# First scatters of a routed expert layer in threes, and a second routing choice made earlier

## The reference, cut to what matters

```
u     = xn2 @ (Ws + Wi).T + bs + bi        # xn2: a second layernorm with weight and bias
h_t   = tanh(h_(t-1) @ A.T + u_t)          # a recurrence of width 16 over 2048 steps
s     = (H @ Wo.T + bo) * sigmoid(xn2 @ Wg.T + bg) + xn
score = sigmoid(xn @ gate_w.T)             # 16 experts
idx   = top4(score + gate_b); w = 2.5 * score[idx] / sum(score[idx])
y     = sum_k w_k * (silu(gate) * up) @ w2[idx_k].T + shared expert(xn)
out   = x + s * silu(y)
```

## Time and profile before

| | us |
|---|---|
| median of three runs | 548.22 |
| lowest, highest run | 541.35, 548.29 |
| the profiled execution, its own time | 537.79 |
| its span, first to last instruction | 535.6 |

### The profile page before, as it was taken

The page is one execution under the profiler, slowest core; times in us unless marked ns, Lnnn a source line. Parts: engine busy times, 40 slices in busy tenths (PEclk is TensorE's granted clock), DMA queues, the critical chain, the costliest instruction groups (busy, mean ns, idle before and its releaser), DMA issues.

```text
span 535.6 us, 11523 instructions
## 1 busy us (share of the span) xinstructions
PE 375.5 (70%) x3635; PEld 294.3 (55%) x3635; DVE 307.3 (57%) x913; ACT 280.8 (52%) x532; POOL 265.5 (50%) x280
## 2 busy tenths in 40 slices
PE   0458357697998988769888898997867778673110
PEld 0344225265887877647666786776756556551000
DVE  4889637277752456523554567776643445456544
ACT  1842548567765454546666677766745444451000
POOL 2007746660005666565665554545456555425774
PEclk9977779699999899888999999999989788787555
DMA  7988967964868897588878898988867777345454
GB/s 243 386 279 306 303 229 227 357 189 132 249 216 258 261 298 224 168 267 253 264 238 280 263 301 279 273 272 262 262 197 249 219 208 217 121 144 165 145 153 129
DMA packets 106569, 127.06 MB, mean 237 GB/s; under 512 B 10257, under 2 KB 95890, under 8 KB 106514
## 3 DMA queue, kind: packets, MB, share of 16 engines
q1 hardware_dynamic: 92544, 92.17, 53.7%
q0 software_dynamic: 12288, 33.57, 20.7%
q10 hardware_dynamic: 1682, 0.59, 0.4%
HBM read 59.71 MB, written 66.58 MB: 236 GB/s over the span
## 4 chain that ended last, share of the span: by engine, by line
PE 40%; issue 13%; DVE 9%; POOL 5%; ACT 5%; another core or an unknown queue 3%; DMA 1%; POOLq 0%; ACTq 0%; DVEq 0%
PE bank L739 16%; PE bank L762 10%; PE bank L563 6%; POOL xn_parts L544 5%; PE bank L752 4%; ACT xn_f L1588 2%; DVE xn_parts L1322 2%; DVE xn_f L1271 1%; DVE sh_h L1277 1%; DVE sh_silu L1285 1%; PE bank L786 1%; ACT xn_f L1596 1%; PE bank L791 1%; PE bank L840 1%
## 5 line engine op out<-in xcount | busy, mean ns | idle before, releaser
L523 POOL DMA_INDIRECT x_slots<-xn_parts,slot_u x128 | 129.2, 1009 | 154.6 <-PE bank L563 67.3
L544 POOL DMA_INDIRECT xn_parts<-y_slots,slot_u x128 | 129.3, 1010 | 108.6 <-PE bank L563 29.5
L739 PE MATMUL bank<-w_all,xn_f 128*128 x1038 | 139.4, 284 | 17.2 <-issue 13.5
L1271 DVE SCALAR_TENSOR_TENSOR xn_f<-bank,xn_f 128x256 f32<-128x256 f32 x88 | 36.9, 419 | 152.0 <-ACT xn_f L1596 90.3
L739 PEld LDWEIGHTS bank<-w_all,xn_f 128*128 128x128 f16 x1038 | 100.7, 102 | 40.5 <-issue 26.7
L1588 ACT ACTIVATE xn_f<-bank 128x1024 f16<-128x1024 f16 x88 | 88.5, 1007 | 26.3 <-remote 15.9
L1612 ACT ACTIVATE y_ring<-bank 128x512 f32<-128x512 f32 x88 | 51.9, 590 | 68.7 <-PE bank L762 40.1
L762 PE MATMUL bank<-w_all,sh_silu 128*128 x519 | 76.5, 285 | 9.2 <-issue 7.3
L563 PE MATMUL bank<-ident_h,w_stage 128*128 128x128 f16 x692 | 56.4, 225 | 2.9 <-issue 1.9
L762 PEld LDWEIGHTS bank<-w_all,sh_silu 128*128 128x128 f16 x519 | 47.8, 103 | 18.7 <-issue 11.8
L1596 ACT ACTIVATE xn_f<-bank 128x256 f32<-128x256 f32 x88 | 33.5, 381 | 44.5 <-remote 21.4
(11 more groups left out here) (173 smaller groups left out, 479.4 us busy)
## 6 DMA issues: line engine op xcount, KB each, us to landing
w_stage<-x_slots SPq DMA_DIRECT2D x85, 256.0 KB
y_slots<-y_ring SPq DMA_DIRECT2D x85, 256.0 KB
x_ring<-in_x SPq DMA_DIRECT2D x32, 256.0 KB
x_slots<-zero_h SPq DMA_DIRECT2D x1, 8064.0 KB, 30.6
x_slots<-zero_h SPq DMA_DIRECT2D x7, 1024.0 KB
x_slots<-zero_h SPq DMA_DIRECT2D x7, 768.0 KB
w_stage<-in_w13t SPq DMA_DIRECT2D x17, 256.0 KB
x_ring<-in_x SPq DMA_DIRECT2D x8, 512.0 KB
```

The source lines that it names most:

```text
L523: eng.indirect_dma_start(out=x_slots[s], out_offset=bass.IndirectOffsetOnAxis(ap=slot_u[:, n * TOPK + k:n * TOPK + k + 1], axis=0), in_=xn ...
L544: eng.indirect_dma_start(out=fin_y[:, r, j, k, :], out_offset=None, in_=y_slots[s], in_offset=bass.IndirectOffsetOnAxis(ap=slot_u[:, n * T ...
L739: mm = eng.matmul(gu[:, j * 2 * F:(j + 1) * 2 * F], xg_T[:, n % 2, ((j * 2 + px) * KD + k) * P:((j * 2 + px) * KD + k + 1) * P], w_all[:, ...
L1271: eng.scalar_tensor_tensor(out=h_sb[:, n % 2, 0:nb, :], in0=gv[:, 0:nb, F:2 * F], scalar=DESCALE, in1=silu_sb[:, n % 2, 0:nb, :], op0=ALU. ...
```

## The change

It does six things. (1) POOL no longer scatters segment 0 tile by tile: the 48 scatters go in sixteen groups of three, and each group but the first waits for a step of a list (`steps`), the last of them `gate_pre` 14. (2) Of the preparation in the head, batch 7 moves one loop later on each engine: x_norm from loop 3 to 4, x_low from 4 to 5, transposes and scoring from 5 to 6. (3) VectorE chooses the experts of group 3 in loops 3 and 4 of the head and of group 4 in loop 5, no longer in slots 3 to 14 of the pairs; only group 5 stays there. (4) Ranks, counts and slots of segment 1 come in slots 7 to 19 and no longer 10 to 25. (5) Scatters of segment 1 start at pair count 9 and spread over 20 counts (before 11 and 17), those of segment 2 at 29 and over 16 (before 28 and 14). (6) Gathers and units move by up to three pairs to later ones, and gathers of segment 1 spread slightly wider.

```diff
--- before.py
+++ after.py
@@ -80,10 +80,13 @@
     FIN_RING = 3
     XF_RING = 2
     XM_RING = 2
-    SCATTER_PAIR = (0, 11, 28)
-    SCATTER_PAIRS = (0, 17, 14)
+    SCATTER_PAIR = (0, 9, 29)
+    SCATTER_PAIRS = (0, 20, 16)
     PIECES = 8
-    GATE_LEAD = 2
+    NORM_AT = {0: 4, 1: 5, 2: 6, 4: 7}
+    LOW_AT = {0: 3, 1: 4, 2: 5, 3: 6, 5: 7}
+    TURN_AT = {1: 3, 2: 4, 3: 5, 4: 6, 6: 7}
+    ROW = 3
 
     ctx = ExitStack()
     with ctx:
@@ -311,9 +314,9 @@
         SCAN0 = [U_SLOT + 4, U_SLOT + 4 + 25]
         OUT_SLOT = 43
         CHECK, FALLBACK, PARTS = U_SLOT + 55, U_SLOT + 59, U_SLOT + 60
-        UNIT_PAIR = (46, 50, 55, 59, 64, 68, 74, 77, 80, 83)
-        GATHER_PAIR = (43, 47, 52, 56, 61, 65, 70, 73, 76, 79, 82, 85)
-        GATHER_PAIRS = (4, 3)
+        UNIT_PAIR = (48, 52, 56, 60, 64, 68, 74, 78, 81, 85)
+        GATHER_PAIR = (45, 49, 53, 57, 61, 65, 70, 74, 77, 81, 84, 88)
+        GATHER_PAIRS = (8, 7)
         UNIT_SLOT = {SLOTS * p: c for c, p in enumerate(UNIT_PAIR)}
         MIX_SLOT = {78 + 6 * c: c for c in range(NU)}
 
@@ -497,16 +500,15 @@
             eng.wait_ge(diagonal, 3)
             eng.memset(shift_f[:, P // SEQS:P // SEQS + N], 0.0).then_inc(shifted, 1)
 
-            def beside_gates(n):
-
-                if n == 1:
-                    eng.wait_ge(sh_silu_done, 1)
-                elif n == 2:
-                    eng.wait_ge(sh_hidden, 1)
-                elif n == 3:
-                    eng.wait_ge(sh_lo, 1)
-                elif n > 3:
-                    eng.wait_ge(gate_pre, n - GATE_LEAD)
+
+            steps = ((sh_silu_done, 1), (sh_hidden, 1), (gate_pre, 2), (x_hi, 5), (gate_pre, 3), (x_hi, 6), (gate_pre, 5),
+                     (x_hi, 7), (gate_pre, 7), (gate_pre, 8), (gate_pre, 9), (gate_pre, 10), (gate_pre, 11),
+                     (gate_pre, 13), (gate_pre, 14))
+
+            def beside_gates(i):
+                if i and i % ROW == 0:
+                    made, count = steps[i // ROW - 1]
+                    eng.wait_ge(made, count)
 
             def slot_x(s):
                 eng.wait_ge(filled[s], 16 * (1, PIECES, PIECES)[s])
@@ -514,9 +516,9 @@
                     if n in GRP0:
                         eng.wait_ge(slots_step, 4 * GRP0.index(n) + 4)
                     b = n // BT
-                    if s == 0:
-                        beside_gates(n)
                     for k in range(TOPK):
+                        if s == 0:
+                            beside_gates(n * TOPK + k)
                         if s:
                             i = (n - TILE0[s]) * TOPK + k
                             eng.wait_ge(pair_t, SCATTER_PAIR[s] + i * SCATTER_PAIRS[s] // (SEG_TILES[s] * TOPK))
@@ -540,7 +542,7 @@
                     n = c * FT + j
                     if c < len(GATHER_PAIR):
                         i = k * FT + j
-                        eng.wait_ge(pair_t, GATHER_PAIR[c] + i * GATHER_PAIRS[s] // (TOPK * FT))
+                        eng.wait_ge(pair_t, min(GATHER_PAIR[c] + i * GATHER_PAIRS[s] // (2 * TOPK * FT), NPAIR))
                     eng.indirect_dma_start(
                         out=fin_y[:, r, j, k, :], out_offset=None, in_=y_slots[s],
                         in_offset=bass.IndirectOffsetOnAxis(ap=slot_u[:, n * TOPK + k:n * TOPK + k + 1], axis=0))\
@@ -690,12 +692,12 @@
             bias_products()
             blocks_ended(0)
             for b in range(NB):
-                if 0 < b < NB - 2:
-                    x_transpose(b + 2)
+                if b in TURN_AT:
+                    x_transpose(TURN_AT[b])
                 shared_up(b)
                 gates(b, 0)
-                if 0 < b < NB - 2:
-                    route_batch(b + 2)
+                if b in TURN_AT:
+                    route_batch(TURN_AT[b])
                 if b < NB - 1:
                     gates(b, 1)
 
@@ -844,14 +846,14 @@
             def beside(slot):
                 if slot == 1:
                     u_transpose()
-                if slot == 10:
+                if slot == 7:
                     rank(3)
-                if slot == 14:
+                if slot == 8:
                     rank(4)
                     block_counts(1)
-                if slot == 16:
+                if slot == 10:
                     block_starts(1)
-                if slot == 23:
+                if slot == 17:
                     blocks_ended(1)
                 if slot == 38:
                     rank(5)
@@ -1195,8 +1197,8 @@
                 if b == 1:
                     norm_stats(6)
                 shared_hidden(b)
-                if b + 3 < NB:
-                    x_low(b + 3)
+                if b in LOW_AT:
+                    x_low(LOW_AT[b])
                 if b == NB - 1:
                     u_ratio(0)
                 gates(b, 0)
@@ -1211,6 +1213,14 @@
                     norm_stats(7)
                     norm_scale(3)
                     norm_ratio(3)
+                if b == 3:
+                    choose_scores(3)
+                    choose_largest(3)
+                    choose_index(3)
+                if b == 4:
+                    choose_marks(3)
+                if b == 5:
+                    choose(4)
             u_ratio(1)
             def pick_weights(i):
                 r = slice(i * GT, (i + 1) * GT)
@@ -1368,26 +1378,25 @@
                     out_weights()
                 if slot == OUT_SLOT + 6:
                     out_bias()
-                for g, first in ((3, 3), (4, 7), (5, 27)):
-                    if slot == first:
-                        choose_scores(g)
-                    if slot == first + (1 if g < 5 else 3):
-                        choose_largest(g)
-                    if slot == first + (3 if g < 5 else 6):
-                        choose_index(g)
-                    if slot == first + (4 if g < 5 else 9):
-                        choose_marks(g)
-                for s, counts in ((1, 15), (2, 39)):
+                if slot == 27:
+                    choose_scores(5)
+                if slot == 30:
+                    choose_largest(5)
+                if slot == 33:
+                    choose_index(5)
+                if slot == 36:
+                    choose_marks(5)
+                for s, counts in ((1, 9), (2, 39)):
                     if slot == counts:
                         block_counts(s)
                     if slot == counts + 2:
                         block_starts(s)
-                for g, first in ((3, 18), (4, 20), (5, 42)):
+                for g, first in ((3, 12), (4, 14), (5, 42)):
                     if slot == first:
                         route_slots(g)
                     if slot == first + 1:
                         route_rows(g)
-                for s, first in ((1, 22), (2, 44)):
+                for s, first in ((1, 16), (2, 44)):
                     if slot == first:
                         blocks_ended(s)
                     if slot == first + 3:
@@ -1544,18 +1553,18 @@
             x_norm(3)
             weights_high(0)
             for b in range(NB):
-                if 0 < b < NB - 2:
-                    x_transposed(b + 2)
-                    x_low_transposed(b + 2)
+                if b in TURN_AT:
+                    x_transposed(TURN_AT[b])
+                    x_low_transposed(TURN_AT[b])
                 shared_up(b)
                 weights_high(2 * b + 1)
                 shared_hidden(b)
-                if 0 < b < NB - 2:
-                    route_batch(b + 2)
+                if b in TURN_AT:
+                    route_batch(TURN_AT[b])
                 weights_high(2 * b + 2)
                 gates(b, 0)
-                if b + 4 < NB:
-                    x_norm(b + 4)
+                if b in NORM_AT:
+                    x_norm(NORM_AT[b])
                 if b < NB - 1:
                     gates(b, 1)
 
```

## The result

| | before | after |
|---|---|---|
| median of four runs each, same chip | 544.79 (540.49 to 548.29) | 521.54 (520.55 to 522.21) |
| ratio, with its 95% interval | | 0.9575 (0.9482 to 0.9668) |
| the profiled execution, its own time | 537.79 | 521.4 |
| its span | 535.6 | 519.1 |

The account below looks back on a forecast made before the run. No single bound: a head, 88 pairs paced mostly by TensorE, then POOL's gathers and the last units. Terms 5 + 2 - 5 - 2 - 1 + 0 = -1 us gave 547.2 on the median, put at 546; range 535 to 557.

Parts of the forecast that it names:

- (a): Handover to the pairs: segment 0's last scatters become late and delay the first load of x slots; +5 us (+3 to +8).
- (c): Head, up to 72 us and 88 to 110: twelve fewer scatters where the standstills lie; -5 us (bounds 0 and -16).
- +2 for the choosing: Head, loops 3 to 6: choosing for groups 3 and 4 partly sticks out, batch 7 moves; +2 us (0 to 4).
- rival 2: Head: both standstills go, 16 us less in place of 5, giving 536; chance 0.13.
- (d): Pairs 3 to 8: the choosing leaves the pairs, so they run faster; -2 us (0 to -2.5).
- (e): Pairs: segment 1's scatters spread over 20 pair counts instead of 17; -1 us (bounds +2 and -14.5).
- Rival 3: Segment 1: density of scatters decides its pace, -14.5 us instead of -1, about 534; chance 0.07.
- (f): Late pairs: gathers and unit slots move later, last unit still fits POOL's idle time; 0 us, up to +2.

Follow-up runs that it names:

- bursts: The changed kernel with the same scatters and gathers over the same pairs, but released eight at a time: 647.56 us, ratio 1.1864.
- the thin ones: The bursts kernel with one eighth of each row moved by its indirect transfers: 641.90 us, ratio 1.1935.

## Why the prediction was wrong, step by step

**(a) to (c), the handover.** The sum came near and its parts did not; that was in part luck. I had +5 for the late scatters, +2 for the choosing, -5 for the stretches, together +2; measured +0.7 (132.94 against 132.21). The gates of batch 6, put at 126.26 and hoped for near 123, end at 118.17 + 0.87 = 119.04: the standstill of 66 to 74 us is gone whole, and the second is shorter by half a us (ACT waits 6.14 us at 100.00, before 6.71). The count that I priced (c) by did not come: by 72 us POOL had started 20 scatters and not 18, and from 88 to 110 it had 13 and not 9. Six scatters left the two stretches instead of twelve, 2.6 us by my price, and the gates came 7.2 us earlier. This was half of rival 2. It did not pay, as POOL issues six scatters in a row until 124.39 and TensorE waits for the load behind them. Of the signs set for (a) one came, the load waits for the scatters; the first pair is 13.9 us behind the gates of batch 6 and not 8 to 11. What the threes are worth in the whole time is not settled to better than some us: 0 to 6 when undone, 0.5 to 5 alone.

**(d), -2.** By the y copies it looks right in its place and lost later: from pair 0 to pair 8 after takes 32.6 us, before 34.2, and after with the choosing in its old slots 35.4. But that kernel has caught up by pair 44 (309.6 in both) and is 2.6 us ahead at pair 84. By the sign that I had set it missed: the first matmuls of pairs 3 and 8 are at 139.04 and 159.89, 4.17 us each, where before had 3.90 and I wanted 3.5. Alone on before the early choosing gives nothing (1.0058).

**(e), -1: this step failed.** Its bounds had +2 and -14.5, and I took -1 since "each scatter keeps its 0.433 wherever it goes". At pair 40 after is 14.6 us ahead of before (10.5 in its second profile); with the old counts it is only 4.1 ahead. Pairs 10 to 26, for which 4.3 us or more was the sign, take (229.21 - 163.56) / 16 = 4.10. Rival 3's size is near what pair 40 shows, though in the whole time the counts are worth 4 to 10 us. Its reason, density on the DMA engines, was not right for the bursts, as the thin ones show. What goes with the gain is that fewer scatters follow without a break.

**(f), 0: this step failed too.** I looked at whether the last unit fits before the handover to segment 2, which it did (POOL waits 11.03 us there, where I had about 3), and costed the spacing of the gathers at nothing. It was the largest part: 11 to 19 us when undone, 1 to 14 alone. I had the gathers as POOL's work off the path, not as what stands beside the stops.

**Behind both stands one reading.** I took the standstills of the head for instructions that arrive late "while the DMA engines are busy", and so priced transfers by the share of sixteen engines that they take. The rows of the head spoke against it and I did not set POOL's rows beside them: before the hole of 66 to 74 us POOL issued scatters without a break from 54.43 to 72.2, fourteen in a row. But the head alone would not have proved it: in after a run of six scatters (77.27 to 85.2) stops nothing, with TensorE busy for 8.07 and ScalarE for 7.85 of the 9 us from 77 to 86.

**The rule that I weighed**, from the Trainium skill, "Runtime: NRT & Kernel Launch", "Instruction fetch mechanics", says that the fetch of instructions stays hidden behind dispatch. By it (c) was 0, and the stops would not be late instructions. The traces lean the same way: in the burst from 183.66 two engines stand 3.38 and 4.12 us with no releaser, and no packet of an instruction queue moves from 185 to 197. My own reading, instructions that arrive late, has no support there. What else the three engines share, that a run on POOL holds up, stays open.

**What is shown and what is not.** Shown: that in the pairs runs of five and more transfers go with pairs of 5 to 13 us, in each profile from a chip where before takes 537 to 545 us; that adding runs adds such pairs (+24% of the time at the same work); that the bytes and the DMA engines' time for them do not matter for that; that breaks of 1.2 us in an otherwise unchanged kernel before give the same 4% as the change; and that gathers and counts carry most of the change's gain. Not shown: the mechanism inside the chip; whether it is the run or POOL's rate alone; how much each part of the change is worth in us; why runs of four, and now and then none at all, go with a long pair; why a run of six in the head stops nothing; why breaks everywhere slow the earlier pairs of the changed kernel; and why one chip is free of it.

## What to carry to other kernels

Where an engine issues indirect transfers beside others' work, put its timeline beside each hole of 5 us and more that "issue" or "remote" ends: rows that all read 0.30 "issue", five or more, are the sign. The DMA share in the hole does not decide it: it was 0.86 in one hole here and 0.26 in another. Cutting the transfers' bytes and timing again does. Then break the runs after three with a wait of about 1.2 us (a memset here), only where the run is, and time it on more than one chip. Two parts of a change that place work on one queue are to be costed together: here the new scatter counts gave nothing without the new gathers.

## What the runs showed of the hardware that was not expected

- A run of eight indirect transfers (10 us of POOL) goes with stops of TensorE, ScalarE and VectorE. In one burst TensorE stood 4.23 us from its fifth transfer on, in the next 3.38 us. A part of the idle time has no releaser in the profile, the rest is one engine's wait for another. A pair of 3.7 us becomes one of 5 to 13.
- It does not depend on the bytes: 647.56 with 33.57 MB and 641.90 with 4.21 MB on that queue (16.0% and 3.6% of the DMA engines' time).
- A break of 1.24 us behind every third transfer takes the time back (544.02 to 522.22); one of 0.5 us does not (536.85 beside 537.18), nor does the long one behind every sixth (536.42, with one run of 527.11).
- A stop can cost a second time, as TensorE's granted clock is 0.50 behind it: twelve matmuls took 2.75 us instead of 1.48.
- A stop of this kind came and went with no packet on an instruction queue (185 to 197 us of bursts).
- The same kernel before took 537 to 545 us on five chips and 460.6 on a sixth. There a profile of the changed kernel with its breaks has runs of 20 and 37 transfers that stopped nothing, and a DMA share of 0.92.
